# Moving the input normalisation and the first weight splits into the block of the layers

## The reference, cut to what matters

```python
xn = (x - mean(x)) / sqrt(var(x) + 1e-5)           # 2 x 1024 x 128
# six layers, on xn
qkv = shift_tokens(xn) @ Wqkv                       # 128 -> 3 x 1024; half of the channels one token back
q, k = l2norm(q) * qs, l2norm(k) * ks               # 16 heads of 64, then rotary position
out = local_attention(q, k, v) @ Wo                 # windows of 32 tokens, each sees itself and the one before
x = x + out
x = x + (a * gelu(gate)) @ W2 + b2                  # after layer norm, shift_tokens and W1
# recurrent branch, on xn
xh = causal_conv(x @ W_in)                          # 4 taps
alpha = exp(-8 * softplus(forget_base) * sigmoid(forget))
h = scan(alpha, sqrt(1 - alpha**2 + 1e-6) * sigmoid(inp) * xh)
```

## Time and profile before

| | |
|---|---|
| time of three runs | 1684.09, 1681.55, 1683.95 us |
| time of the profiled execution | 1679.53 us |
| its span (first to last instruction) | 1677.7 us |
| granted TensorE clock, mean | 0.995 |
| busy share of PE, DVE, ACT, POOL | 95%, 82%, 81%, 79% |
| DMA moved | 156.91 MB, mean 94 GB/s |

### The profile page before, as it was taken

How to read it: one execution, slowest core, us unless ns; L and a number is a source line. 1 busy time by engine, 2 the same in 40 slices (tenths; PEclk the granted TensorE clock), 3 DMA queues, 4 the chain that set the end, 5 groups by cost and what they waited for, 6 DMA issues and landing times. The chain is left out here.

```text
span 1677.7 us, 50128 instructions
## 1 busy us (share of the span) xinstructions
PE 1599.8 (95%) x19920; PEld 1371.0 (82%) x19920; DVE 1367.4 (82%) x2005; ACT 1350.7 (81%) x2517; POOL 1327.0 (79%) x1276
## 2 busy tenths in 40 slices
PE   4799999999999999999999999999999999999985
PEld 2588888888888888888888888888888888788773
DVE  5888888888888888888888888888888877888833
ACT  3578888888888888888888888888888888888874
POOL 8888888888889888889888889888888777666630
PEclk9999999999999999999999999999999999999997
DMA  5233332433423434333344233343342332222220
GB/s 182 72 104 95 101 93 72 131 88 111 108 72 91 110 103 118 92 87 93 90 123 117 77 103 88 88 130 100 86 110 68 85 87 76 71 67 68 68 85 29
DMA packets 184947, 156.91 MB, mean 94 GB/s; under 512 B 111502, under 2 KB 156172, under 8 KB 184716
## 3 DMA queue, kind: packets, MB, share of 16 engines
q1 hardware_dynamic: 184716, 153.70, 32.7%
HBM read 27.30 MB, written 1.05 MB: 17 GB/s over the span
## 5 line engine op out<-in xcount | busy, mean ns | idle before, releaser
L1492 POOL TENSOR_TENSOR qk<-qk,t 128x1024 f32<-128x1024 f32 x192 | 456.2, 2378 | 96.4 <-DVE qk L1265 96.4
L1262 DVE TENSOR_TENSOR t<-ps_qn,tab 128x512 f32<-128x512 f32 x384 | 264.4, 688 | 136.0 <-ACT sq L1018 125.2
L1504 POOL TENSOR_TENSOR qkr<-qk,rinv 128x1024 f32<-128x1024 f32 x192 | 361.8, 1906 | 7.7 <-PE ps_tr L753 0.4
L740 PE MATMUL ps_qn<-w_hi,xs_hi 128*128 128x512 f32 x576 | 260.3, 452 | 21.3 <-POOL xs_lo L1540 10.3
L1005 ACT ACTIVATE pbd<-ps_tr 64x512 f32<-64x512 f32 x384 | 226.1, 589 | 62.8 <-PE ps_tr L753 60.0
L1018 ACT ACTIVATE sq<-ps_qn 128x512 f32<-128x512 f32 x384 | 229.0, 597 | 46.7 <-PE ps_qn L742 41.9
L1265 DVE TENSOR_TENSOR qk<-ps_qn,tab 128x512 f32<-128x512 f32 x384 | 261.0, 680 | 0.0
L1054 ACT ACTIVATE qbd<-ps_tr 64x512 f32<-64x512 f32 x384 | 227.1, 591 | 33.5 <-PE ps_tr L766 28.1
L741 PE MATMUL ps_qn<-w_lo,xs_hi 128*128 128x512 f32 x576 | 229.7, 399 | 0.0
L742 PE MATMUL ps_qn<-w_hi,xs_lo 128*128 128x512 f32 x576 | 229.1, 398 | 0.0
L1275 DVE TENSOR_REDUCE ss<-sq 128x32 f32<-128x2048 f32 x96 | 216.6, 2257 | 0.0
(11 more groups left out here) (153 smaller groups left out, 3223.0 us busy)
## 6 DMA issues: line engine op xcount, KB each, us to landing
v_own<-v_new SPq DMA_DIRECT2D x96, 512.0 KB, 3.3
v_back<-v_new SPq DMA_DIRECT2D x96, 384.0 KB, 3.5
v_back<-v_own SPq DMA_DIRECT2D x96, 128.0 KB, 2.3
kT<-kT SPq DMA_DIRECT2D x84, 128.0 KB, 2.7
w_raw<-in_Wqkv SPq DMA_DIRECT2D x18, 512.0 KB, 5.3
rot<-in_rot SPq DMA_DIRECT2D x48, 128.0 KB, 2.6
xsh<-x SPq DMA_DIRECT2D x192, 32.0 KB, 2.7
fx<-xmid SPq DMA_DIRECT2D x96, 64.0 KB, 2.1
```

The source lines that it names most:

```text
L740: mm(ps_qn[bank][:, :], xs_hi[b][:, :], w_hi[:, part], start=True, stop=False)
L1262: v.tensor_tensor(t2[:, part].rearrange("p (h s d) -> p h s d", s=2, d=DH // 2), swapped, tab[:, 2 * k + 1:2 * k + 2, :].rearrange("p o (s ...
L1492: g.tensor_tensor(qk[b][:, part], qk[b][:, part], t2[:, part], ALU.add).then_inc(added[b], 1)
L1504: g.tensor_tensor(qkr[b][:, part].rearrange("p (h d) -> p h d", d=DH), qk[b][:, part].rearrange("p (h d) -> p h d", d=DH), rinv[b][:, k * ...
```

## The change

The block `normalise` is gone; its work is spread over the first halves of the layers' block.

- Tiles 0 and 1 of both streams (4 columns of statistics, `HEAD`) are normalised ahead of half (0, 0); the other 12 have their statistics on DVE in (0, 0), their root in (0, 1), and are normalised by ACT in three groups of four at the end of (0, 1), in the middle of (1, 0) and at the end of (1, 0). PE transposes them in (1, 0) and (1, 1), DVE copies them into `x`.
- `xs_hi` and `xs_lo` of half (0, 0) are made straight from `x` by two half-height instructions each, on ACT and DVE, without a DMA.
- The weights of layer 0 are split in 512-column pieces: the high part on ACT, the low part on POOL, each with a semaphore that PE waits for by chunk.
- `evac_v` of steps 0 and 1 is on ACT.
- POOL clears less (not `v_own`, `v_back`, and of `kT` only the first window). The mask constants are made after `low_x` in (0, 0); four small instructions of softplus, `centre_w` and the clearing of the recurrent weights after `low_x` in (0, 1); the series of softplus, 21 instructions on 128x2 elements, after `low_x` in (2, 0).
- ACT waits for `rec_par` ahead of half (0, 0). Its DMA is the fifteenth that SP issues.
- The eight DMAs for the recurrent branch are issued in half (3, 0) instead of (1, 0).

```diff
-        normalise(nc, a, x, xmid, branch, ident, eps_col, s_const, w, rec)
-        layers(nc, a, x, xmid, branch, ident, w, rec)
+        layers(nc, a, x, xmid, branch, ident, eps_col, w, rec)
...
 SP:
-                    if (i.n, b) == (1, 0):
+                    if (i.n, b) == (0, 1):
+                        w.load_first(sp)
+                    if (i.n, b) == (3, 0):
+                        sp.wait_ge(s_xT, 6)
+                        sp.wait_ge(rec_cleared, 1)
                         sp.dma_start(branch[:, :, LEAD:], x[:, :, 1:]).then_inc(branch_in, 16)
...
+                load_x(0, 2, 0)
+                sp.dma_start(ident[:, :], a["ident"]).then_inc(s_const, 16)
+                w.load_wqkv(sp, 0, 0)
+                w.load_rot(sp, 0)
+                w.load_scales(sp, 0)
+                load_x(2, 5, 1)
+                w.load_wqkv(sp, 0, 1)
+                w.load_wqkv(sp, 0, 2)
+                load_x(5, TILES, 2)
                 sp.dma_start(fc[:, :, :], a["mask"]).then_inc(mask_in, 16)
                 sp.dma_start(fsq[:, 0, :], a["sel"]).then_inc(mask_in, 16)
+                sp.dma_start(rec.par[:, :, :], a["rec_par"]).then_inc(rec_par_in, 16)
...
 ACT:
+                    if (i.n, b) == (1, 0):
+                        normalise_pair(1)
+                        softplus_exp()
...
+                    if i.n < 2:
+                        evac_v(i, b, 4)
+                        evac_v(i, b, 5)
+                    if (i.n, b) in ((0, 1), (1, 0)):
+                        normalise_pair(2 * i.n)
+
+                nc.scalar.preload_act_table_set("natural_log_exp_and_others")
+                act.wait_ge(s_set, 4)
+                input_guess(0)
+                split_first(0)
+                normalise(range(1))
+                split_first(1)
+                normalise(range(1, 2))
+                round_first_x()
+                normalise(range(2, HEAD))
+                split_first(2)
+                split_first(3)
+                act.wait_ge(rec_par_in, 16)
+                f(rec.half_b[:, :, :], rec.par[:, :, 5:7], ACT.Copy, scale=0.5)
...
 DVE:
+                input_stats(range(HEAD), 0)
+                input_moments(range(HEAD), HEAD)
+                input_root(0)
+                copy_head(0, 1)
+                copy_head(1, 2)
+                low_first_x()
+                input_stats(range(HEAD, 10), 1)
...
 POOL:
+                    if (i.n, b) == (0, 0):
+                        mask_constants_bf()
+                    if (i.n, b) == (0, 1):
+                        softplus_size()
+                        clear_recurrent()
+                    if (i.n, b) == (2, 0):
+                        softplus()
...
+                clear()
+                split_first(0)
+                split_first(1)
                 tables(Step(0, 0))
-                low_x(Step(0, 0), 0)
-                for piece in range(2):
-                    w.split_high(g.tensor_copy, pool, 0, 2, piece)
-                    w.split_low(g, pool, 0, 2, piece)
+                for c in range(2, 6):
+                    split_first(c)
```

More of the change, by code:

```diff
@@ L195 @@
     w_out: object
[L198 to L329, removed]
-                act.wait_ge(s_nw, 5)
-                for t in range(NT):
-                    s.activation(xt(t), xt(t), ACT.Identity, bias=shift[:, t:t + 1], scale=rstd[:, t:t + 1]).then_inc(s_xn, 1)
-                    if t == B:
-                        act.wait_ge(soft, 2)
-                        s.activation(e, size, ACT.Exp, scale=-1.0).then_inc(soft_exp, 1)
-                        s.activation(e_sb[:, :, :], size, ACT.Exp, scale=-1.0).then_inc(soft_exp, 1)
-            @block.tensor
-            def _(pe):
-                pe.wait_ge(s_const, 16)
-                for t in range(NT):
-                    pe.wait_ge(s_xn, t + 1)
-                    m = nc.tensor.transpose(ps[:, t // 4, (t % 4) * P:(t % 4 + 1) * P], xt(t), ident[:, :])
-                    if t % 4 == 3:
-                        m.then_inc(s_tr, 1)
@@ L458, in load_first @@
     def load_first(sp):
-        for part in range(3):
-            load_wqkv(sp, 0, part)
         load_wo(sp, 0)
@@ L613, in shift_x @@
                 def shift_x(t, b):
-                    if not valid(t):
+                    if not valid(t) or (t.first and b == 0):
                         return
+                    if t.n < TILES:
+                        sp.wait_ge(s_xT, b + 1 if t.n == 0 else 3 + t.n // 2)
                     after_first(sp, xs_ready[b], t.n, t)
@@ L761, in transpose_qk @@
                     pe.wait_ge(qk_ready[b], 2 * j.n + (1 if k else 2))
+                    if j.first and b == 0:
+                        pe.wait_ge(s_nw, 10)
                     for f in (2 * k, 2 * k + 1):
@@ L940, in rec_output, with transpose_input, transpose_pair @@
                     last.then_inc(qn_full[bank], 1)
+                def transpose_input(columns, bank):
+                    for n, c in enumerate(columns):
+                        pe.wait_ge(s_xn, c + 1)
+                        tr(bank[:, n * P:(n + 1) * P], in_tile(c), ident[:, :]).then_inc(s_tr, 1)
+                def transpose_pair(r):
+                    pe.wait_ge(s_xT, 2 + r)
+                    transpose_input(range(HEAD * (r + 1), HEAD * (r + 2)), in_pair(r)[0])
                 def half(i, b):
@@ L948, in half @@
                     qkv(i, b, (2, 3))
+                    if i.first and b == 0:
+                        pe.wait_ge(s_xT, 1)
+                        transpose_input(range(B, HEAD), ps_pv[0])
+                    if (i.n, b) == (1, 0):
+                        transpose_pair(0)
                     if b == 0:
@@ L1415, in rec_scan, with input_stats, input_moments @@
                         v.tensor_tensor_scan(h[:, c, :], decay[:, c, :], h[:, c, :], first, ALU.mult, ALU.add).then_inc(rec_h, 1)
+                def input_stats(columns, part):
+                    for c in columns:
+                        dve.wait_ge(x_in[part], 32)
+                        v.bn_stats(stats[:, c, :], in_tile(c)).then_inc(s_st, 1)
+                def input_moments(columns, done):
+                    dve.wait_ge(s_st, done)
+                    for c in columns:
+                        v.bn_aggr(mv[:, c, :], stats[:, c, :]).then_inc(s_st, 1)
@@ L1422, in half @@
                         rotate(i, b, c)
+                        if i.first and (b, c) == (1, 1):
+                            input_root(1)
+                        if i.first and (b, c) == (0, 3):
+                            copy_head(B, HEAD)
+                    if (i.n, b) == (1, 1):
+                        copy_pair(1)
+                        softplus_recip()
                     row_sums(*soft)
@@ L1425, in half @@
                     rec_conv1d(i, b)
-                    if b == 0:
+                    if i.first and b == 0:
+                        square_sums(i, b)
+                        input_stats(range(10, COLUMNS), 2)
+                        input_moments(range(HEAD, COLUMNS), HEAD + COLUMNS)
+                    elif (i.n, b) == (1, 0):
+                        square_sums(i, b)
+                        copy_pair(0)
+                    elif b == 0:
                         square_sums(i, b)
```

225 lines of the change are left out of this document (197 added, 28 removed).

## The result

| | median us | runs | lowest to highest |
|---|---|---|---|
| before | 1682.3 | 5 | 1681.55 to 1684.09 |
| changed | 1691.57 | 5 | 1690.87 to 1695.76 |

The ratio is 1.0056, 95% interval 1.0042 to 1.0071: slower by some 9 us, where 1685.0 was forecast with a range to 1689.5.

What follows compares the result with a forecast made beforehand. No single engine was taken as the bound, but a POOL, ACT and DVE loop without slack between `xs_lo` and `floored`. 13.4 - 0.7 - 2.8 - 2.1 - 5.9 - 2.9 = -1.0, so 1683.95 + 1.0 = 1685.0 us, range 1679.5 to 1689.5.

Steps and rivals of the forecast that it cites:

- (a): Half (0, 0): the mask constants, now made behind `xs_lo`, give back 0.7 us.
- (b): Half (0, 1), POOL between `xs_lo` and `floored`: small softplus instructions, `centre_w` and clearing give back 2.8 us.
- (c): ACT in half (1, 0): eight normalises, an exponential and two v copies exceed its idle time and give back 2.1 us.
- (d): Half (2, 0): 21 dependent small softplus instructions on POOL give back 5.9 us.
- a lead below -5 after (3, 1): Sign of being wrong: after half (3, 1) the changed kernel runs more than 5 us later than before.
- ScalarE stood idle 8.15 us for `floored` in (2, 1): Sign of being wrong: no ACT idle time before `floored` in (2, 1); about 8 us of idling was forecast.
- Lead 13.4. This holds if nothing stalls.: Start: `xs_lo` of half (0, 1) runs 13.4 us earlier than before (the lead), at 21.6 against 35.03.
- rival 2: Start stalls on `rec_par`, the fifteenth DMA, issued late by a full queue; lead falls 2.7 to 3.6, 1688.0 us; chance 0.17.
- No cover: 5.9: Half (2, 0): POOL's idle 1.08 hides none of the 21 softplus instructions, so all 5.9 us count; upper bound 6.5.
- (e): SP in half (3, 0): eight DMAs issued ahead of `carry_k` delay it; ACT stalls 4.7, and 2.9 us is given back.
- Rival 3: Half (3, 0): the DMA burst fills the queue, `kT` takes 5.4 instead of 2.7 to land, 1687.7 us; chance 0.13.
- if the early ones stay slow for longer, POOL covers it: Start: should PE's early matmuls stay slow for longer, POOL hides that until half (1, 0), at no cost.

Runs made afterwards that it cites:

- k4: The changed kernel with ScalarE's wait for `rec_par` and the one operation behind it moved from the start to step 30; 1690.46 us, ratio 1.0046.
- k1: The changed kernel with 60 extra unread matmuls where TensorE only waits, in (1, 0), (2, 1) and (3, 0); 1687.63 us, ratio 1.0029.
- k6: The changed kernel with `rec_par` wait, recurrent DMAs and softplus series moved later, and the (0, 1) clearing and softplus block cut into twelve pieces; 1672.06 us, ratio 0.9936.

## Why the prediction was wrong

Its loop and its places were right, and so were the sizes of (a), (b) and, as work alone, (c) and (d). The sum was wrong by 11.3 us in the second profile (-12.3 against -1.0). Of its own signs of being wrong, one came (a lead below -5 after (3, 1)) and one did not (ScalarE stood idle 8.15 us for `floored` in (2, 1), about 8 as forecast). By terms:

1. **"Lead 13.4. This holds if nothing stalls."** It stalled: 3.4 us. This is rival 2, in the place it named; its limit, a landing later than 12.3, was passed by 3 us. It was wrong only on how: the issue was not held up, it came at 9.47 and took 0.46; the landing took long. That the 3.62 before meant a full queue is shown by no run. With the wait moved (k4) the lead is 13.0, so the rest of the start's working holds. The chance of 0.17 was too low for a load that is fifteenth and has a waiter ahead of the first square.
2. **(a), (b)** measured 0.6 and 2.8: right.
3. **(c) 2.1 and (d) 5.9** are right as work (2.2 and 6.0 in k1), and 1.9 and 1.8 short as losses. The step that failed is "No cover: 5.9": I took the loss as the length of the block, and never asked what TensorE does in a pause of 6 us. The upper bound of 6.5 was built from POOL's rows alone, so it left out another engine's reaction.
4. **(e) 2.9** was 7.1: 2.0 to 2.5 of it clock (k1), 1.7 to 2.2 a term mis-sized. I subtracted 1.77 that `evac_q` had to spare. From the start of `evac_k` to that of `evac_q` it is 3.61 before, 3.75 in the changed kernel and 2.89 in k1: the cover gave nothing in the one and 0.7 in the other, since TensorE's work for `evac_q` comes behind the `fsq` of the same late ScalarE (the pause of 4.87). And ScalarE stood longer for kT than 4.7: 5.74, and 5.14 in k1. I also took `move_v` to fit in the same delay; in k1, DVE waits 1.36 for `v_own` at 134.28. Rival 3, a kT that lands late, did not occur (2.6 us). Its price was near, its mechanism not: rivals 2 and 3 together would have given 1690.7, and that this lies near 1691.57 would be luck.
5. The start's 3.4, the clock's 5.7 to 6.2 and (e)'s 2.2 to 1.7 make 11.3.

One line of the prediction touches it: "if the early ones stay slow for longer, POOL covers it". That was thought of for the start and not for the pauses later on. The Trainium skill, "TensorE: Matmul & The Clock Gate", Part 1 "The HAM clock gate", says that the clock is set by how busy TensorE has been lately. The rows agree: it fell at the pauses of 4.58, 6.18 and 4.87 us, and stayed at 1.00 where k1 filled the last two. Of the ramp at the start of a kernel the same part says that it is under 1% of a typical span and that a model should not fit the count of slow matmuls. For these pauses the share is as small (6.2 of 1692 is 0.4%), and it is still about two thirds of what this change lost by the medians.

## What to carry to other kernels

Price a block that is put on the critical loop as its length plus what the pause behind it costs on TensorE: here about 2 us for each pause of 4.6 to 6.2 us, over a loop of which TensorE is 95% busy. Cut such blocks into pieces and put them where the engine waits anyway (k6: 25 small operations and eight pieces of clearing at no cost). In a queue that issues in order, look first at what stands behind a burst: the same eight DMAs cost 7 us ahead of the loads of this half that others wait for, clock included, and nothing behind them.
